# Masking the transposed scores of a windowed attention after a copy, by affine selection on POOL, in place of mask matmuls on TensorE

## The reference

```python
q = apply_rope(proj(Wq, bq)) * Dh ** (-0.5)
k = apply_rope(proj(Wk, bk))
v = proj(Wv, bv)
scores = einsum('bhqd,bhkd->bhqk', q, k)
rel = idx[None, :] - idx[:, None]                # key minus query
blocked = (rel > 0) | (rel < -128)
scores = where(blocked[None, None], -inf, scores)
out = einsum('bhqk,bhkd->bhqd', softmax(scores), v)
x = layernorm(x + out @ Wo.T + bo)
```

## Time and profile before

| | us |
|---|---|
| median of 3 runs (2842.92 to 2848.92) | 2846.15 |
| profiled execution | 2839.36 |
| its span in the trace | 2837.5 |
| first layer, from its first transposes to its last store | about 15 to 1080 |
| first to last "tr" mask matmul | 94.1 to 1055.4 |

### The profile page before, as it was taken

How to read it: one execution, slowest core, us unless ns; L and a number is a source line. 1 busy time by engine, 2 the same in 40 slices (tenths; PEclk the granted TensorE clock), 3 DMA queues, 4 the chain that set the end, 5 groups by cost and what they waited for, 6 DMA issues and landing times. The chain is left out here.

```text
span 2837.5 us, 44896 instructions
## 1 busy us (share of the span) xinstructions
PE 2315.9 (82%) x18544; PEld 1432.9 (50%) x18544; DVE 1485.0 (52%) x2615; ACT 886.6 (31%) x1257; POOL 677.7 (24%) x404
## 2 busy tenths in 40 slices
PE   2899999999999985677675598894598898889896
PEld 1455555555555455565563266553355555555553
DVE  2445555555555544455454165547556756766662
ACT  0233333333333333333341121220143333334332
POOL 4121112221111201131431433433102113202212
PEclk7899999999999997898888799997699999999997
DMA  6455664555565404675676210102443244235230
GB/s 144 93 105 111 118 123 99 114 113 104 114 117 115 98 24 148 221 257 178 212 240 208 78 60 30 60 30 66 143 129 97 78 144 144 73 103 159 84 91 16
DMA packets 227353, 329.19 MB, mean 116 GB/s; under 512 B 15072, under 2 KB 164944, under 8 KB 226896
## 3 DMA queue, kind: packets, MB, share of 16 engines
q1 hardware_dynamic: 224336, 325.68, 43.0%
q10 hardware_dynamic: 2816, 0.65, 0.1%
HBM read 197.71 MB, written 127.93 MB: 115 GB/s over the span
## 5 line engine op out<-in xcount | busy, mean ns | idle before, releaser
L1678 ACT ACTIVATE l1f_probs<-l1f_slot 128x1024 f32<-128x1024 f32 x240 | 240.6, 1022 | 423.1 <-PE l1f_slot L1851 252.3
L518 DVE TENSOR_REDUCE l0a_rowmax<-l0a_slot 128x4 f32<-128x1024 f32 (+1 forms) x256 | 293.4, 1156 | 128.4 <-PE l0a_slot L631 125.5
L461 ACT ACTIVATE l0a_probs<-l0a_slot 128x1024 f32<-128x1024 f32 (+1 forms) x256 | 248.4, 971 | 338.0 <-PE l0a_slot L621 189.0
L1741 DVE TENSOR_REDUCE l1f_rowmax<-l1f_slot 128x1 f32<-128x1024 f32 x240 | 287.6, 1219 | 100.5 <-PE l1f_slot L1837 100.3
L1851 PE MATMUL l1f_slot<-l1f_Qs,l1f_Ks 128*128 128x256 f32 x960 | 184.5, 319 | 42.9 <-DVE l1f_rowmax L1741 16.8
L1851 PEld LDWEIGHTS l1f_slot<-l1f_Qs,l1f_Ks 128*128 128x128 f32 x960 | 141.6, 200 | 113.2 <-ACT l1f_probs L1678 30.3
L1837 PE MATMUL l1f_slot<-l1f_Ks,l1f_Qs 96*128 96x512 f32 x480 | 170.7, 449 | 29.2 <-DMA l1f_Qs<-kq_rows 12.7
L421 POOL TENSOR_TENSOR l0a_turned<-l0a_turned 128x512 f32<-128x512 f32 x32 | 40.7, 1272 | 560.8 <-DVE l0a_turned L504 560.8
L621 PE MATMUL l0a_slot<-l0a_mask,l0a_ident 128*128 128x512 bf16 (+1 forms) x512 | 150.4, 376 | 25.7 <-issue 23.4
L1796 PE MATMUL l1f_os<-l1f_probs,l1f_V 128*32 128x256 f32 x1920 | 165.8, 398 | 1.8 <-ACT l1f_probs L1678 0.9
L563 PE MATMUL l0a_O<-l0a_probs,l0a_V 128*32 128x128 f32 x3840 | 156.5, 279 | 10.6 <-issue 10.6
(11 more groups left out here) (190 smaller groups left out, 4069.3 us busy)
## 6 DMA issues: line engine op xcount, KB each, us to landing
expert_outputs<-l0f_inter SPq DMA_DIRECT2D x64, 512.0 KB, 3.7
l0f_wide<-expert_outputs SPq DMA_DIRECT2D x32, 1024.0 KB, 10.2
l0a_Qs<-qk_rows SPq DMA_DIRECT2D x96, 256.0 KB, 7.8
l0a_Ks<-qk_rows SPq DMA_DIRECT2D x96, 256.0 KB, 14.8
l1f_Ks<-kq_rows SPq DMA_DIRECT2D x48, 512.0 KB, 6.7
qk_rows<-l0a_hi SPq DMA_DIRECT2D x32, 512.0 KB, 2.8
qk_rows<-l0a_lo SPq DMA_DIRECT2D x32, 512.0 KB, 4.2
l0f_f<-in_dram SPq DMA_DIRECT2D x32, 512.0 KB, 5.1
```

The lines of the kernel that those rows point to most:

```text
L461: exp_ready.by(act.activation(probs[:, t % 2, HG * g:HG * g + HG, 0:reach, :], s[:, :, 0:reach, :], ACT.Exp, scale=SCALE))
L518: max_ready.by(dve.reduce_max(rowmax[:, t, :, 2 * g:2 * g + 2], s[:, :, :, first:2 * P], AX))
L1678: exp_done.by(act.activation(probs[:, half, u - FIRST[i], :], s[:, :], ACT.Exp, scale=SCALE))
L1741: max_done.by(dve.reduce_max(rowmax[:, 2 * u + t:2 * u + t + 1], s[:, :], AX))
```

## The change

The "tr" steps have no mask matmuls any more. ACT copies the raw scores from PSUM to `probs`; POOL overwrites the blocked elements with -1e30 by two `affine_select` instructions in place (keys after the query in the own tile, keys before the window in the next tile; the last tile of a sequence has only the first); ACT then takes the exponential in place. The exponential is a new step, "exp", placed behind the next "tr" step of the tile, and for the tile's last group at the head of the next pv part. A PSUM tile of "tr" is released by the copy (`copied`) and no longer by the exponential. "nat" keeps its mask. The table `maskT` is no longer loaded.

```diff
+    BLOCKED = -1e30
     for i in range(BT):
...
+        steps += [(0, "exp", NHG * i + NHG - 1)]
         steps += merged([(0, "pv", NHG * i + g) for g in range(NHG)], [(on, "nat", NHG * tn + g) for g in range(NHG)],
                         begun.get(i, []))
         steps += [(0, "oT", i)]
-        steps += merged([(ot, "tr", NHG * tt + g) for g in range(NHG)], [(on, "maxT", tn), (on, "place", tn), (0, "back", i)], front[i])
+        rows = merged([(ot, "tr", NHG * tt + g) for g in range(NHG)], [(on, "maxT", tn), (on, "place", tn), (0, "back", i)], front[i])
+        for step in rows:
+            steps += [step] + ([(ot, "exp", step[2] - 1)] if step[1] == "tr" and step[2] % NHG else [])
...
-            return [{"nat": (max_ready, n + 1), "maxT": (maxT_ready, n + 1), "tr": (exp_ready, n + 1),
+            return [{"nat": (max_ready, n + 1), "maxT": (maxT_ready, n + 1), "tr": (copied, n + 1),
...
# POOL
+                if kind == "tr":
+                    t, g = i // NHG, i % NHG
+                    copied.wait(pool, X, i + 1)
+                    alone_here = bool(n and t == BT - 1)
+                    for a, sign in enumerate((1,) if alone_here else (1, -1)):
+                        part = probs[:, t % 2, HG * g:HG * g + HG, a, :]
+                        pool.affine_select(part, part, [[0, HG], [sign, P]], ALU.is_ge, BLOCKED, base=0, channel_multiplier=-sign)                            .then_inc(cut.sem, 2 if alone_here else 1)
...
# ACT
                     pv_done.wait(act, X if t else X - 1, NHG * ((t - 1) % BT) + g + 1)
                     reach = 1 if n and t == BT - 1 else 2
-                    exp_ready.by(act.activation(probs[:, t % 2, HG * g:HG * g + HG, 0:reach, :], s[:, :, 0:reach, :],
-                                                ACT.Exp, scale=SCALE))
+                    copied.by(act.copy(probs[:, t % 2, HG * g:HG * g + HG, 0:reach, :], s[:, :, 0:reach, :]))
+                if kind == "exp":
+                    t, g = i // NHG, i % NHG
+                    part = probs[:, t % 2, HG * g:HG * g + HG, 0:1 if n and t == BT - 1 else 2, :]
+                    cut.wait(act, X, 2 * i + 2)
+                    exp_ready.by(act.activation(part, part, ACT.Exp, scale=SCALE))
...
# TensorE
-                    mask_ends = bool(kind == "tr" and g % 2)
...
-                    if not mask_ends:
-                        add_mask()
+                    if kind == "nat":
                         for half in range(2):
+                            mm(o[:, half, :, reach, :], ident16[:, :], mask[:, reach, :].unsqueeze(1).broadcast_to([P, 2, wide, P]),
+                               start=True, stop=False, skip_group_check=True)
                     for j in range(2):
                         for half in range(2):
                             r = slice(HALF * half, HALF * half + rows)
                             last = mm(o[:, half, j, reach, :].rearrange("p a q -> p (a q)"), left[r, 2 * g + j, here],
-                                      right[r, 2 * g + j, moving], start=mask_ends and not j, stop=not mask_ends,
+                                      right[r, 2 * g + j, moving], start=kind == "tr", stop=True,
                                       skip_group_check=True, tile_position=(HALF * half, 0))
-                    if mask_ends:
-                        last = add_mask()
```

More of the change, by code:

```diff
@@ L287, in window_attention_layer @@
         mask = sb("mask", [P, 2, P], bf16)
-        maskT = sb("maskT", [P, 2, P], bf16)
         wq = sb("wq", [P, CH, D]); wk = sb("wk", [P, CH, D]); wv = sb("wv", [P, CH, D]); wo = sb("wo", [P, CH, D])
@@ L327, in window_attention_layer @@
         placed = [signal(f"placed{t}", BT, 16) for t in range(2)]
-        exp_ready = signal("exp_ready", BT * NHG); pv_done = signal("pv_done", BT * NHG)
+        copied = signal("copied", BT * NHG); exp_ready = signal("exp_ready", BT * NHG); cut = signal("cut", 2 * BT * NHG); pv_done = signal("pv_done", BT * NHG)
         oT_ready = signal("oT_ready", BT); recip_ready = signal("recip_ready", BT); ao_ready = signal("ao_ready", BT)
@@ L338, in window_attention_layer @@
         schedule.signals(filled, reader)
-        NCONST = 12 + 2 * HR
+        NCONST = 11 + 2 * HR
         NSETUP = 8
@@ L351, in _ @@
                 sp.dma_start(dst[:, :], src).then_inc(consts, 16)
-            for dst, src in ((mask, mask_in), (maskT, maskT_in)):
-                sp.dma_start(dst[:, :, :], src.rearrange("p (a n) -> p a n", a=2)).then_inc(consts, 16)
+            sp.dma_start(mask[:, :, :], mask_in.rearrange("p (a n) -> p a n", a=2)).then_inc(consts, 16)
             for dst, src in ((as_given[0], wq_in), (as_given[1], wk_in), (wv[:, :, :], wvT), (wo[:, :, :], woT)):
@@ L404, in _ @@
         def _(pool):
-            for s in (biased, rot_ready, lo_ready):
+            for s in (biased, rot_ready, lo_ready, cut):
                 s.start(pool)
@@ L436, in _ @@
         def _(act):
-            for s in (xT_ready, hi_ready, exp_ready, oT_ready, aoT_ready, *placed):
+            for s in (xT_ready, hi_ready, copied, exp_ready, oT_ready, aoT_ready, *placed):
                 s.start(act)
@@ L609, in piece @@
                         reach = slice(0 if tile else 1, 2)
-                        rows, table, left, right = ROWS, mask, Qs, Ks
+                        rows, left, right = ROWS, Qs, Ks
                         moving = slice(P * (tile - 1 + reach.start), P * tile + P)
@@ L613, in piece @@
                         reach = slice(0, 2 if tile < NT - 1 else 1)
-                        rows, table, left, right = ROWS + 1, maskT, Ks, Qs
+                        rows, left, right = ROWS + 1, Ks, Qs
                         moving = slice(P * tile, P * (tile + reach.stop))
                     wide = reach.stop - reach.start
-                    mask_ends = bool(kind == "tr" and g % 2)
-                    def add_mask():
+                    if kind == "nat":
                         for half in range(2):
[L621 to L624, removed]
-                    if not mask_ends:
-                        add_mask()
+                            mm(o[:, half, :, reach, :], ident16[:, :], mask[:, reach, :].unsqueeze(1).broadcast_to([P, 2, wide, P]),
+                               start=True, stop=False, skip_group_check=True)
                     for j in range(2):
```

## The result

The changed kernel takes 2911.81 us (median of 4 runs, 2904.07 to 2932.86), the kernel before beside it 2845.21. The ratio is 1.0242, 95% interval 1.0213 to 1.0271: slower by 67 us.

A forecast was written before the change was run, and what follows sets the result against it. TensorE was taken to set the pace by a small margin; new waits through ACT and POOL, less saved masks, summed to 7.4 us a block, +115 us over 15.5 blocks, forecast 2960 us; 8-in-10 range 2835 to 3130.

The forecast's parts named there:

- The dearer selection: On POOL, each affine selection of 128x512 taken at 1.25 us, range 0.6 to 2.4, two for each "tr".
- the masks' saving: On TensorE, removed "tr" masks worth 6.4 us a block, of which 4.8 are left after the wait for DVE.
- my chains: Waits through ACT and POOL, net per block: tile 0 +1.6 us, tile 1 +3.9, tile 2 +1.6, tile 3 +0.3.
- rival 3: POOL's selections at the copy's 0.6 us: savings and ACT's chain nearly cancel, +10 us, 2856; chance 0.07.
- rival 4: TensorE's clock falls in one part of each block, in tiles 1 and 2: +93 us on top, 3050; chance 0.05.
- signs of being wrong: Selection under 0.6 or over 1.8 us, TensorE idle near 4 us a block, or granted clock below 1.00.
- The part about maxT: First "tr" of tiles 1 to 3 gives nothing: maxT waits for DVE, done about 1.4 us into the part.
- rival 2: TensorE stays the bound, faster, at "tr" 1 to 3 of each tile: 74 us saved, 2772; chance 0.16.
- Rival 1: POOL becomes the bound by its sum, selections at 2.4 us: 85 us a block, about 3190; chance 0.12.
- pv waiting for the exponential: In tiles 1 and 2, last pv needs exp 3: +3.9 us in tile 1, +3.7 in tile 2's full-width passes.
- cut 1 behind k's rotations: Tile 1 on POOL: k's rotations end at 9.2 us, so the selections of "tr" 1 end at 11.8.
- table load: ACT reloading tables, 1.28 us each time, as copy and exponential alternate; ruled out, since the trace has one load.

The follow-up runs named there:

- a3: The kernel before without the transposed scores' masks and nothing in their place (exponential at 1/64 scale, keys unmasked): 2835.49 us, ratio 0.9974.
- a5: The kernel of a3 with masks left in 6 of a block's 16 transposed-score steps, where TensorE would wait anyway: 2809.82 us, ratio 0.9884.
- b2: The changed kernel with POOL's rotations of q and k moved behind the selections of the part: 2900.76 us, ratio 1.0208.
- b3: The changed kernel with ACT copying xT before the exponentials of groups 0 and 1 in tile 0: 2893.61 us, ratio 1.0188.
- b1: The changed kernel with masks put back in 9 of a block's 16 transposed-score steps, in front of waits: 2906.27 us, ratio 1.0238.
- b5: The changed kernel with the order changes of b2 and b3 and masks back in the same 6 steps as a5: 2873.16 us, ratio 1.0100.
- a4: The kernel before without transposed-score masks; POOL selects after the exponential, which is straight from PSUM at 1/64 scale: 2840.09 us, ratio 0.9983.
- a8: The kernel of a4 with masks put back in the same 6 steps a block as in a5: 2815.70 us, ratio 0.9884.

## Why the prediction was right, and where it wasn't

Slower was right, and so was its cause: the chain through ACT and POOL costs 73 to 76 us with the masks or without. That the size, 67 us where I said 115, came out inside the range is in good part luck, since two terms of the sum were wrong in opposite ways. The dearer selection had put some 105 us too much into it, the masks' saving had taken some 65 too much out. With both put right my sum gives about 115 - 105 + 65 = 75 us, a rough figure, since the terms are not quite independent.

*The selection.* I took 1.25 us, between rows of the same shape with arithmetic in them; it is 0.61. This is the mis-sized term. The nearest row was the copy, 0.61 for 512 elements, which I had put down as the bound from below. The sentence of the Trainium skill (GPSIMD Engine Reference, Engine selection) that one-input operations run at roughly line rate agrees with this row; TENSOR_SCALAR at 1.48 stays the exception to it.

*The sum at that price.* With 0.6 us my chains gave 0.7 us a block, 10 us in all (rival 3). Measured are 4.1 a block. By parts, in the block from 500.78 us: q starts 508.03 - 500.78 = 7.25 us into tile 0's part, 7.0 before, so the chain costs 0.25 there, where I had 1.6 with the dearer selection; tile 1 from its first "tr" to tile 2's takes 537.02 - 520.53 = 16.5 us, 15.7 before, +0.8; tile 2 takes 551.63 - 537.02 = 14.6 as before; tile 3 takes 570.33 - 551.63 = 18.7, 16.1 before, +2.6, of which v, 6.1 in place of 3.7, is 2.4. So the waits alone, 1.2 us in this block, stay near the chains at that price. The rest is q's length, 6.5 in place of 3.6, and v's: the clock. Both are slow in this block, which is why it is longer, at 69.6 us, than the mean of 65.7.

*The clock.* I had it as rival 4, with a chance of 0.05 and a price added on top of the forecast, in the pv parts of tiles 1 and 2, and a granted clock below 1.00 was one of my signs of being wrong. That sign came: 0.93. The clock fell mainly in q and v, and not in every block (q's mean of 766 ns lies three tenths of the way from 592 to 1193); these two made 2.6 us a block, and the pv parts added something. I had also counted TensorE busy for 52 us of about 70; it was 54.2 of 65.7.

*What the masks give.* The 4.8 us a block was the other term that failed. The part about maxT was right and too small: its waits grew from 15.0 to 48.3 us, and from 37 to 54 in number, since tile 0's maxT waits now too. But a3, with nothing added, kept 10 us, not 75. I had not followed what stands behind "tr" 1 and 2 of tile 1: "back" waited already 1.1 us for DVE there, and the two saved masks went into that wait, 15.1 to 31.4 us. The clock took more: a5, with more work, is 26 us faster than a3. Even a5, at nearly the full clock, keeps 33 us only, and its longer waits for ACT's exponential show where more of the saving goes. So rival 2, faster by 74 us, was out of reach for the change as made: with nothing at all added on ACT and POOL it would have been faster by a quarter of a per cent.

*Slips in the working.* A block takes 61.6 us and not 63.0; my 252 us held a little more than four. By the 0.43 us that I took for a pair of masks, the three first "tr" cost 1.3 and leave 5.1 us, not 4.8 (which follows from the 0.53). Rival 1 could not decide from 1.8 us by my own lines: POOL's sum is 67 us there, the chains give about 80. None of them changes the forecast's sense.

*The waits forecast.* ACT waiting for POOL, pv waiting for the exponential, cut 1 behind k's rotations: all there, and b2 and b3 price POOL's order and ACT's order in tile 0 at 11 us (within the noise) and 18. POOL never came near its sum (rival 1), and no table load was added.

Open is how the 76 us of the chain divide between waits and clock in the changed kernel. The clock's 2.6 us a block in q and v are lengths of matmuls, not a price: b1 raises the clock to 0.98 and gains nothing, because the time turns into waits for ACT. b1 and b5 raise the clock only by adding work, so they do not measure it by itself. No run made the transposed scores' mask cheaper and kept the result: a4 and a8 only show what such a form would be worth.

## What to carry to other kernels

Work that is taken from the busiest engine is worth only what does not land in a wait behind it: list for each removed instruction what the engine waits for next, before multiplying. On TensorE the holes have a second price, the clock, and then leaving some of the removed work in front of those waits can be faster than leaving none (a5 against a3), as long as no other engine's chain binds (b1 gained nothing). And an engine with idle time is not free if the pass put on it stands in the middle of another's chain: the same 480 selections cost 34 us between ACT's copy and its exponential, and nothing that can be told behind them.

## What the hardware showed that I had not expected

- POOL's affine selection, 128x512 in float32 and in place: 0.64 us mean, 0.61 in pairs; TENSOR_SCALAR of the same shape 1.48.
- TensorE's clock fell to the 1.2 GHz level again and again inside a layer where it was busy for 82% of the time (727 of 882 us), with no wait longer than 2.2 us, and stayed at 2.4 GHz in the kernel before, where it was busy for 93%: the same q matmul took 592 ns at one level and up to 1193 at the other. What it did before a fall: busy 3.5 of 6 us in the changed kernel, 2.0 of 4 in a3.
- ACT's exponential from and to SBUF takes 1.06 us for 128x1024, out of PSUM 1.02; the copy out of PSUM 1.01.
